# A decoder layer on one core: the q and k tables with the heads innermost, their low parts made later, and the routing spread out

## The reference

```python
# self attention: 16 heads of 8, relative logits from the unscaled queries
qkv = x @ qkv_w.T + qkv_b
logits = einsum('bhqd,bhkd->bhqk', q, k) * scale
pos = _rel_pos_logits(q_pos, rel_emb)            # [B*H, L, L], masked beyond +-99
out = einsum('bhqk,bhkd->bhqd', softmax(logits + pos), v) @ proj_w.T + proj_b
# cross attention: causal, k and v from ctx_1024, no biases
# experts: 64, top 8 of 4 kept groups of 8, relu(x @ up)^2 @ down, and a shared expert
x = layernorm(x + self_attention(x))
x = layernorm(x + cross_attention(x, ctx_1024))
x = layernorm(x + routed_experts(x) + shared_expert(x))
```

## Time and profile before

| What | Value |
|---|---|
| Median of 3 runs | 346.91 us |
| The profiled execution: time | 344.19 us |
| The profiled execution: span, first to last instruction | 342.4 us |
| Mean granted TensorE clock | 0.915 of 2.4 GHz |
| Busy: PE, DVE, ACT, POOL | 267.5, 228.3, 207.3, 141.0 us |
| Chain that ended last, by engine | PE 41%, DVE 18%, SP queue 12%, DMA 11%, issue 7%, POOL 5%, ACT 4% |
| Bytes moved | 41.09 MB in 55683 packets, of them 9.18 MB written to HBM |

### The profile page before, as it was taken

How to read it: one execution, slowest core, us unless ns; L and a number is a source line. 1 busy time by engine, 2 the same in 40 slices (tenths; PEclk the granted TensorE clock), 3 DMA queues, 4 the chain that set the end, 5 groups by cost and what they waited for, 6 DMA issues and landing times.

```text
span 342.4 us, 6024 instructions
## 1 busy us (share of the span) xinstructions
PE 267.5 (78%) x1904; PEld 210.6 (62%) x1904; DVE 228.3 (67%) x571; ACT 207.3 (61%) x573; POOL 141.0 (41%) x139
## 2 busy tenths in 40 slices
PE   2919999893069999998778775649969599999991
PEld 2608999572057887665555443538747488878870
DVE  2697854663038888986659989449999745674533
ACT  1502362774018888898767863346666578878861
POOL 7560000600000012244443500227569589879990
PEclk9976999998569999999989987688989899999997
DMA  6522225733432333465554100099547267658501
GB/s 113 144 97 104 102 103 180 172 83 130 154 105 64 94 94 92 93 158 149 149 167 136 50 0 3 15 225 253 138 124 171 73 163 179 174 160 215 142 0 31
DMA packets 55683, 41.09 MB, mean 120 GB/s; under 512 B 15394, under 2 KB 44772, under 8 KB 55652
## 3 DMA queue, kind: packets, MB, share of 16 engines
q1 hardware_dynamic: 55652, 40.71, 43.7%
HBM read 31.52 MB, written 9.18 MB: 119 GB/s over the span
## 4 chain that ended last, share of the span: by engine, by line
PE 41%; DVE 18%; SPq 12%; DMA 11%; issue 7%; POOL 5%; ACT 4%; POOLq 0%; DVEq 0%; ACTq 0%
PE bank L683 14%; PE bank L667 9%; SPq L417 6%; DMA qc_dram<-q_lo 5%; POOL unit_lo L594 5%; PE bank L718 4%; PE bank L700 4%; DVE spread L1086 3%; SPq L398 2%; DMA k_bd<-k_dram 2%; SPq L413 2%; PE bank L728 2%; DVE scaled L1262 2%; PE bank L706 2%; PE bank L739 1%
## 5 line engine op out<-in xcount | busy, mean ns | idle before, releaser
L594 POOL TENSOR_TENSOR unit_lo<-unit,unit_hi 128x512 fp32r<-128x512 f32 x68 | 87.3, 1303 | 48.7 <-ACT unit_hi L993 47.5
L916 ACT ACTIVATE probs<-bank,neg_max 128x128 f32<-128x128 f32 x256 | 72.3, 390 | 29.1 <-DVE neg_max L1123 28.1
L1262 DVE SCALAR_TENSOR_TENSOR scaled<-bank,roots 128x512 f32<-128x512 f32 x64 | 43.4, 686 | 30.2 <-PE bank L683 22.5
L1123 DVE TENSOR_REDUCE neg_max<-bank 128x4 f32<-128x512 f32 x64 | 42.9, 683 | 29.6 <-PE bank L706 29.0
L992 ACT ACTIVATE unit<-scaled 128x512 f32<-128x512 f32 x68 | 42.7, 628 | 32.8 <-DVE scaled L1262 30.5
L718 PE MATMUL bank<-ident,probs 128*128 128x128 f32 x256 | 39.9, 279 | 3.3 <-DVE probs_t L1130 2.4
L993 ACT ACTIVATE unit_hi<-scaled 128x512 fp32r<-128x512 f32 x68 | 41.9, 616 | 0.0
L718 PEld LDWEIGHTS bank<-ident,probs 128*128 128x128 f32 x256 | 30.5, 145 | 10.5 <-issue 5.2
L561 POOL CAST q_hi<-q_t 128x128 fp32r<-128x128 f32 x8 | 2.3, 293 | 83.6 <-ACT q_t L963 83.6
L706 PE MATMUL bank<-k_bd,q_stk 128*128 128x512 f32 x64 | 34.6, 540 | 0.0
L1130 DVE COPY probs_t<-bank 128x512 f32<-128x512 f32 x40 | 27.5, 687 | 10.4 <-PE bank L718 9.7
(11 more groups left out here) (176 smaller groups left out, 480.6 us busy)
## 6 DMA issues: line engine op xcount, KB each, us to landing
roots<-root_dram SPq DMA_DIRECT2D x64, 256.0 KB, 4.6
q_stk<-q_dram SPq DMA_DIRECT2D x8, 256.0 KB, 3.6
k_bd<-k_dram SPq DMA_DIRECT2D x32, 64.0 KB, 3.0
incoming<-in_L_ffn_up_w SPq DMA_DIRECT2D x4, 512.0 KB, 5.3
q_stk<-qc_dram SPq DMA_DIRECT2D x8, 256.0 KB, 3.0
k_bd<-kc_dram SPq DMA_DIRECT2D x32, 64.0 KB, 2.4
incoming<-in_L_ffn_down_w SPq DMA_DIRECT2D x4, 512.0 KB, 4.8
q_dram<-q_hi SPq DMA_DIRECT2D x4, 256.0 KB
```

Of the source, the lines that this page charges most:

```text
L594: nc.gpsimd.tensor_tensor(unit_lo[:, k % R], unit[:, k % 3], unit_hi[:, k % R], ALU.subtract).then_inc(lo_ready, 1)
L916: last = nc.scalar.activation(probs[:, U % 3, h4 * L:(h4 + 1) * L], ps[BS[U % 3]][:, h4 * L:(h4 + 1) * L], ACT.Exp, bias=neg_max[:, U % 4, ...
L1123: nc.vector.tensor_reduce(neg_max[:, U % 4, :], ps[BS[U % 3]][:, :].rearrange("p (h j) -> p h j", h=GH), AX.X, ALU.max, negate=True).then_ ...
L1262: ins = nc.vector.scalar_tensor_tensor(scaled[:, k % 3], h, 0.0, roots[:, n % ROOT_RING, c % ROOTS], ALU.max, ALU.mult)
```

## The change

**Order of the rows.** The 128 output features of q and k were ordered (head within group, feature, group). They are now ordered (feature, head within group, group), so that in the tables the 16 heads stand innermost. The reordering copies of weights, biases, masks and embeddings take the same elements in another order.

**Tables.** The tables of q are now (2, 128, tokens) and those of k (4, 128, tokens): q's parts are stored once each, not twice, and each store writes 128 plain rows. A gather reads q in two DMAs of 64 rows into the two halves of `q_stk`, and k in four DMAs, each into every fourth partition of `k_bd`.

**Who splits, and when.** ScalarE makes the high parts of the self stage for all columns after its last copy of the preparation (`q_high`, `k_high`). GpSimd makes the low parts, also for all columns at once, and first waits for `spread_ready` to reach 2, that is for the parts 0 and 1 of `q_spread`. The stores wait for these, one whole table after the other; the gather of sequence 0 waits for all.

**SyncE's list.** Gather 2 stands before the two loads of pieces. The stores of the context keys stand behind gather 3 (high parts) and gather 4 (low parts), no longer before gather 3.

**Routing.** Batch 2 gets 1.2 parts per step in place of 1.75, batch 3 starts four steps later, and the second turning of weights comes one step after the last part, not two: step 96 in place of 93.

```diff
-BATCHES = [(range(0, 2), 2), (range(2, 4), 3.5), (range(4, 6), 1.75), (range(6, 8), 1.2)]
+BATCHES = [(range(0, 2), 2), (range(2, 4), 3.5), (range(4, 6), 1.2), (range(6, 8), 1.2)]
+ROUTE0[3] += NG
-CT = [ROOTS_AT[1], ROOTS_AT[3] + 2]
+CT = [ROOTS_AT[1], ROOTS_AT[3] + 1]
...
-        q_dram, k_dram, qc_dram, kc_dram = (
-            nc.dram_tensor(f"{n}_dram", (GH, REPS, HD * NG, NB * L), F32, kind="Internal").ap()
-            for n in ("q", "k", "qc", "kc"))
+        q_dram, qc_dram = (nc.dram_tensor(f"{n}_dram", (2, D, NB * L), F32, kind="Internal").ap() for n in ("q", "qc"))
+        k_dram, kc_dram = (nc.dram_tensor(f"{n}_dram", (REPS, D, NB * L), F32, kind="Internal").ap() for n in ("k", "kc"))
...
-            def keep(store, parts, cols, kept):
-                for part, what in enumerate(parts):
-                    sp.dma_start(store[:, part, :, cols], what[:, cols]).then_inc(kept, 16)
-            def keep_queries(store, hi, lo, cols, kept):
-                keep(store, (hi, lo, hi, lo), cols, kept)
-            def keep_keys(store, hi, lo, cols, kept):
-                keep(store, (hi, hi, lo, lo), cols, kept)
+            def keep(store, parts, what, cols, kept):
+                for part in parts:
+                    sp.dma_start(store[part, :, cols], what[:, cols]).then_inc(kept, 16)
...
-                sp.dma_start(q_stk[r][:, :, :].bitcast(F32),
-                             queries[:, :, :, cols].rearrange("h s (d g) t -> (h s d) g t", g=NG))\
-                    .then_inc(stack_here[r], 16)
+                for rep in range(2):
+                    sp.dma_start(q_stk[r][rep * 64:(rep + 1) * 64, :, :].bitcast(F32),
+                                 queries[:, :, cols].rearrange("s (d h g) t -> (s d h) g t", h=GH, g=NG))\
+                        .then_inc(stack_here[r], 16)
                 for h4 in range(GH):
-                    sp.dma_start(k_bd[r][ROWS * h4:ROWS * (h4 + 1), :, h4, :].bitcast(F32),
-                                 keys[h4, :, :, cols].rearrange("s (d g) t -> (s d) g t", g=NG))\
+                    sp.dma_start(k_bd[r][h4::GH, :, h4, :].bitcast(F32),
+                                 keys[:, :, cols].rearrange("s (d h g) t -> h (s d) g t", h=GH, g=NG)[h4])\
                         .then_inc(stack_here[r], 16)
...
-            for f in range(2):
-                cols = slice(f * HT, (f + 1) * HT)
-                sp.wait_ge(q_split, 2 * (f + 1))
-                keep_queries(q_dram, q_hi, q_lo, cols, q_kept[f])
-                sp.wait_ge(k_split, 2 * (f + 1))
-                keep_keys(k_dram, k_hi, k_t, cols, k_kept[f])
-            sp.wait_ge(q_kept[0], 16 * REPS)
-            sp.wait_ge(k_kept[0], 16 * REPS)
+            every = slice(0, NB * L)
+            sp.wait_ge(q_high, 1)
+            keep(q_dram, (0,), q_hi, every, q_kept)
+            sp.wait_ge(k_high, 1)
+            keep(k_dram, (0, 1), k_hi, every, k_kept)
+            sp.wait_ge(q_split, 1)
+            keep(q_dram, (1,), q_lo, every, q_kept)
+            sp.wait_ge(k_split, 1)
+            keep(k_dram, (2, 3), k_t, every, k_kept)
+            sp.wait_ge(q_kept, 16 * 2)
+            sp.wait_ge(k_kept, 16 * REPS)
             sp.wait_ge(zeroed, 2)
             gather(0)
             gather(1)
             sp.wait_ge(zeroed, 3)
+            gather(2)
             load_piece(0)
             load_piece(1)
-            gather(2)
-            sp.wait_ge(q_kept[1], 16 * REPS)
-            sp.wait_ge(k_kept[1], 16 * REPS)
-            sp.wait_ge(k_split, 6)
-            keep_keys(kc_dram, k_hi, kc_t, slice(0, NB * L), kc_kept)
             for B in range(RING, 2 * NB):
...
-                    sp.wait_ge(qc_kept[B % 2], 16 * REPS * ((B - NB) // 2 + 1))
+                    sp.wait_ge(qc_kept[B % 2], 16 * 2 * ((B - NB) // 2 + 1))
                 gather(B)
+                if B == RING:
+                    sp.wait_ge(k_split, 3)
+                    keep(kc_dram, (0, 1), k_hi, every, kc_kept)
+                if B == RING + 1:
+                    keep(kc_dram, (2, 3), kc_t, every, kc_kept)
                 if 0 <= B - 7 < NB:
                     b = B - 7
+                    cols = slice(b * L, (b + 1) * L)
                     sp.wait_ge(qc_split, 2 * (b + 1))
-                    keep_queries(qc_dram, q_hi, q_lo, slice(b * L, (b + 1) * L), qc_kept[b % 2])
+                    keep(qc_dram, (0,), q_hi, cols, qc_kept[b % 2])
+                    keep(qc_dram, (1,), q_lo, cols, qc_kept[b % 2])
...
+            pool.wait_ge(spread_ready, 2)
+            pool.wait_ge(q_high, 1)
+            nc.gpsimd.tensor_tensor(q_lo[:, :].bitcast(F32R), q_t[:, :], q_hi[:, :], ALU.subtract).then_inc(q_split, 1)
+            pool.wait_ge(k_high, 1)
+            nc.gpsimd.tensor_tensor(k_t[:, :].bitcast(F32R), k_t[:, :], k_hi[:, :], ALU.subtract).then_inc(k_split, 1)
...
+            act.wait_ge(out_a, out_count("k1", False))
+            nc.scalar.copy(q_hi[:, :].bitcast(F32R), q_t[:, :]).then_inc(q_high, 1)
+            nc.scalar.copy(k_hi[:, :].bitcast(F32R), k_t[:, :]).then_inc(k_high, 1)
```

More of the change, by code:

```diff
@@ L296, in decoder_layer @@
         qc_split = sem("qc_split")
-        k_kept = [sem(f"k_kept{n}") for n in range(2)]
-        q_kept = [sem(f"q_kept{n}") for n in range(2)]
+        k_kept = sem("k_kept")
+        q_kept = sem("q_kept")
+        q_high = sem("q_high")
+        k_high = sem("k_high")
         qc_kept = [sem(f"qc_kept{n}") for n in range(2)]
@@ L523, in _ @@
             nc.gpsimd.memset(glist[:, :, TOPG:8], -3.0e38).then_inc(consts_made, 1)
-            for f in range(2):
-                cols = slice(f * HT, (f + 1) * HT)
-                pool.wait_ge(out_a, out_count(f"q{f}", False))
-                nc.gpsimd.tensor_copy(q_hi[:, cols].bitcast(F32R), q_t[:, cols]).then_inc(q_split, 1)
-                pool.wait_ge(q_split, 2 * f + 1)
-                nc.gpsimd.tensor_tensor(q_lo[:, cols].bitcast(F32R), q_t[:, cols], q_hi[:, cols], ALU.subtract)\
-                    .then_inc(q_split, 1)
-                pool.wait_ge(out_a, out_count(f"k{f}", False))
-                nc.gpsimd.tensor_copy(k_hi[:, cols].bitcast(F32R), k_t[:, cols]).then_inc(k_split, 1)
-                pool.wait_ge(k_split, 2 * f + 1)
-                nc.gpsimd.tensor_tensor(k_t[:, cols].bitcast(F32R), k_t[:, cols], k_hi[:, cols], ALU.subtract)\
-                    .then_inc(k_split, 1)
+            pool.wait_ge(spread_ready, 2)
[3 more added lines that the diff above has]
+            nc.gpsimd.tensor_tensor(k_t[:, :].bitcast(F32R), k_t[:, :], k_hi[:, :], ALU.subtract).then_inc(k_split, 1)
             pool.wait_ge(ld["x0"], 16)
@@ L546, in _ @@
             pool.wait_ge(out_a, sum(not by_vector(t) for t in TASKS))
-            for f in range(2):
-                pool.wait_ge(k_kept[f], 16 * REPS)
+            pool.wait_ge(k_kept, 16 * REPS)
             nc.gpsimd.tensor_copy(k_hi[:, :].bitcast(F32R), kc_t[:, :]).then_inc(k_split, 1)
-            pool.wait_ge(k_split, 5)
+            pool.wait_ge(k_split, 2)
             nc.gpsimd.tensor_tensor(kc_t[:, :].bitcast(F32R), kc_t[:, :], k_hi[:, :], ALU.subtract).then_inc(k_split, 1)
@@ L558, in _ @@
                     if b == 0:
-                        for f in range(2):
-                            pool.wait_ge(q_kept[f], 16 * REPS)
+                        pool.wait_ge(q_kept, 16 * 2)
                     nc.gpsimd.tensor_copy(q_hi[:, cols].bitcast(F32R), q_t[:, cols]).then_inc(qc_split, 1)
@@ L694, in scores @@
                 if g == 0:
-                    pe.wait_ge(stack_here[r], 16 * (1 + GH) * (B // RING + 1))
+                    pe.wait_ge(stack_here[r], 16 * (2 + GH) * (B // RING + 1))
                 if U < NU:
@@ L890, in _ @@
             for c in range(2):
-                nc.scalar.copy(wc_t[:, c, :].rearrange("p (h d g) -> p h d g", h=GH, g=NG),
-                               done("w_cross")[:, c * D:(c + 1) * D].rearrange("p (h g d) -> p h d g", h=GH, g=NG))
+                nc.scalar.copy(wc_t[:, c, :].rearrange("p (d h) -> p h d", h=H),
+                               done("w_cross")[:, c * D:(c + 1) * D].rearrange("p (h d) -> p h d", h=H))
             nc.scalar.copy(wc_t[:, 2:4, :].rearrange("p c d -> p (c d)"), done("w_cross")[:, 2 * D:4 * D])\
@@ L904, in _ @@
                                    done(f"bias{n}").rearrange("p (i r) -> p r i", i=4)).then_inc(out_a, 1)
-            for f in range(2):
-                act.wait_ge(k_kept[f], 16 * REPS)
+            act.wait_ge(k_kept, 16 * REPS)
             nc.scalar.mul(kc_t[:, 0:HT], done("kc0"), SCALE).then_inc(out_a, 1)
@@ L961, in queries_out @@
                     if b == 0:
-                        act.wait_ge(q_split, 4)
+                        act.wait_ge(q_split, 1)
                     nc.scalar.copy(q_t[:, b * L:(b + 1) * L], ps[BX][:, 0:L]).then_inc(qc_out, 1)
```

22 lines of the change are left out of this document (10 added, 12 removed).

## The result

The changed kernel takes 315.14 us (median of 4 runs, 313.45 to 316.58) against 346.72 (median of 4, 345.05 to 347.46) for the kernel before: a ratio of 0.9094, interval 0.9036 to 0.9151. The prediction was 312, with a range of 303 to 325. The profiled execution took 316.58 (span 314.8), so between the two profiled executions the difference is 27.6 us; in the medians it is 31.6. The medians given for a run are of all its executions; the ratios leave out an execution over 1.5% above its kernel's fastest, so a ratio need not be the quotient of two medians.

The account below looks back on a forecast made before the run. It took the kernel as bound by a slow start, a stop at 79 to 97 us, cross-stage rounds and VectorE's routing; 10.1 + 18.5 + 5.1 + 1.0 = 34.7 us off 346.9 gave 312 us, range 303 to 325.

Parts of the forecast that it names:

- Low parts later: Start: part 0 of `q_spread` falls to 4.28 us without GpSimd beside it, bias tasks begin at 20.3 to 20.4; gain 10.1 us.
- The added wait: Start: stores and gather 0 move later, stores at 250 GB/s, gather 0 lands at 43.4 us; nothing lost.
- My other end: Bound for the start's stores: at 104 GB/s they last 30 us, gather 0 lands near 60.4, taking back 9 us.
- Context keys: Stop from 79 to 97 us goes with the key stores behind gathers 3 and 4; gain 18.5 us.
- The cross stage: Units 40 to 56: rounds of 7.0 to 7.2 us, last store landing in 2.7 us; gain 5.1 us.
- Units 56 to 63: Stretch behind the cross stage's unit 56, without a term of its own in the prediction; change 0.
- Routing spread out: Experts: last root at least 2.8 us later, dense rest 4.3 us shorter; gain 1.0 us taken.
- Slow stores: Rival: stores stay at 104 GB/s, rows spread no wider; gain 18 in all, 329 us; chance 0.09.
- slow gather: Rival: gather of k into every fourth partition runs on one DMA engine, 26 GB/s; 362 us; chance 0.04.
- a part 0 that stays long: Rival at the start: part 0 of `q_spread` stays at 12 us for reasons other than GpSimd; 320 us; chance 0.03.
- The landing: Rival in the cross stage: last store's landing stays at 3.75 us, round 8.0, gain 1.5; 316 us; chance 0.11.
- Roots: Rival in the experts: second half's roots miss unit 36 by 3 us; 315 us; chance 0.05.

Follow-up runs that it names:

- the old plan: Changed kernel with the earlier kernel's routing (batch 2 at 1.75 parts per step, batch 3 not shifted, turn at step 93): 313.62 us, ratio 0.9076.
- the keys first: Changed kernel with both context-key stores put back ahead of gather 3: 315.93 us, ratio 0.9136.
- the best version: Changed kernel with the earlier routing of batches 2 and 3, turn at step 93, and batch 0 one step later: 310.97 us, repeated at 312.72 us.
- the later slot: Changed kernel with batch 0 of the routing one step later, all work kept: 313.28 us, ratio 0.9031.

## Why the prediction was right, point by point

*Low parts later: right (10.1 predicted, 9.65 measured).* The wait alone in the kernel before gives the same 4.30 us. The bias tasks began 1.0 us later than the 20.35 of my sum: the four early products took 3.65 us, not 2.74 (2.51 to 3.75 in the profiled runs made here), and TensorE waited 1.01 us for `ctx_t`, where I had counted 0.68. The bias tasks themselves then took 0.44 less, 28.85 for 29.29. Part 2 of `q_spread` was stretched by 0.97 us to 5.26, where I had 1.4, and hidden.

*The added wait: right in kind, the rate mis-sized.* I took 250 GB/s from loads and gathers; the stores ran at 386 to 445, four times the 104 of before. Gather 0 was issued at 32.5, not 37. It cost nothing either way. My other end, 9 us taken back at 104 GB/s, was for the 3.1 MB of the changed kernel. The experiment with the wait alone has 4.2 MB to store, and there the first scores came 11.1 us later although the bias tasks began 9.7 earlier: 20.8 taken back, of which the megabyte more is 10 by an estimate at 104 GB/s. No run had the narrow stores with 3.1 MB. The Trainium skill's rule of the largest divisor ("DMA: Bandwidth & Descriptors", "Why a DMA increments its semaphore by 16 and not by 1") gave 4 and 16 engines, and 2 and 9 tenths agree with it.

*Context keys: right (18.5 predicted, 18.9 measured).* But of the two edits that I put together here, the width is enough for most: 14.9 us in the kernel before, and only 1.5 us come back when the keys' place is undone. What the place would do without the width is open.

*The cross stage: right (5.1 predicted; 5.5 measured from unit 40 to 56, with 0.3 lost ahead of it), with the landing of the last store mis-sized.* I took 2.7 us between bounds of 2.2 and 3.75 and measured 1.71 to 1.77, below the lower one. It changed nothing, since the round was by then that of TensorE and ScalarE, busy 26.7 and 26.5 of the 28.96 us (VectorE 23.0): 6.76 and 7.03 us for the first two rounds, 7.97 for the last. The section "Anatomy of one DMA" of the Trainium skill ("DMA: Bandwidth & Descriptors"), with about 2 us of fixed time, was nearer than my row, though it too lies a little above. That section is written for DMAs that GpSimd issues; these are SyncE's.

*Units 56 to 63: missed (0 predicted, 3.0 lost).* The step that failed stands nowhere in the prediction as a term: I counted the cross stage to unit 56 and let the rest follow. I had asked of each faster piece what comes late next, but not what it now meets. SyncE loads a weight piece after most rounds, and with SyncE's rounds no longer the bound the loads come earlier against the units: that of piece 7 was issued 0.6 us behind unit 56 (182.95) and is now issued 2.9 us ahead of it (145.80). Its split then lay 6.8 us behind unit 56 and stretched `x_tok`'s affine step, with no TensorE wait on that step; now it lies 2.8 us behind and stretches the first routing step, in front of `o_norm`, which TensorE waits for. Taking the split away gives 2.6 us of the 3.0 back. Moving the routing by one slot gives 3.7, more than was lost, which fits a wait of TensorE for gather 15 in the kernel before (1.93 us) that is gone now. That is shown for the stretch. Of the 19.3 us about 2.3 go with the clock behind the hold, by the run with the old plan, which had the hold at a clock of 1.00.

*Routing spread out: wrong sign (gain 1.0 predicted, 2.8 lost).* The last root came 5.6 us later, the upper end of 2.8 + 4 x 0.7: 3.6 us more VectorE time, 2.8 of them the four units, and 2.2 more idle (in windows 0.2 longer). The tail was to be 4.3 shorter and was 2.8 shorter. Of the missing 1.5, TensorE's clock behind the longer wait for the last root makes 1.05: 2.1 us more at half speed. Of the 2.8, spreading itself costs 0.8 by the run with the old plan; the other 2 come with either plan, and their cause is open. The step that failed is the assumption that VectorE's own work and at most 0.7 us for each meeting with GpSimd set the time to the last root, with the tail shorter by all three steps.

Sum: 9.65 + 18.9 + 5.1 - 3.0 - 0.25 - 2.8 = 27.6. My profiled forecast was 309.5 and the profiled execution took 316.58; the median came to 315.14, 3.1 above the 312, because this time the profiled execution is the slowest of the runs, not the fastest.

*The rivals.* Slow stores, slow gather and a part 0 that stays long are excluded by the rows above. The gather of k into every fourth partition lands in 2.4 us (median of 32), not 3.0, and in the cross stage in 2.6, where it was 2.4. The landing did not stay at 3.75. Roots were not late.

## What to carry to other kernels

Look for stores at a flat rate with few DMA engines busy. Here stores with 4 rows outermost ran at 99 to 106 GB/s with 2 tenths busy, and those with 128 rows at 386 to 445 with 9 tenths; widen such stores first. Then work that had to be done early can be done late, and an edit that loses alone can win with others: the wait alone made the kernel 2.8% slower, the whole change 9% faster. When a stage gets faster, list what is issued from the same queue (here the loads of weight pieces, and so their splits on GpSimd), and see which instructions of the other engines each of those now meets.

## What the hardware showed that I had not expected

- Stores from SBUF to HBM on 16 engines run at 386 to 445 GB/s, against 225 to 292 for this kernel's gathers and loads.
- A `TENSOR_SCALAR` of VectorE that is issued during a GpSimd `TENSOR_TENSOR` or cast lasts until that one ends, in every instance looked at here: `r_one` ended at 153.90, the split of piece 7 at 153.82, 2.14 us for 0.22 of work. In the kernel before, the split of piece 6 (180.36, 2.36 us) held `x_tok`'s step (181.10, 1.71 us), ends at 182.72 and 182.81, and that of piece 7 the next one. `r_one` at 0.84 and 1.15 us in other runs is the same, only issued later: its ends follow those of the cast and the split by 0.08 us. So do the 16 steps of part 0 in the kernel before (the view of the tile `spread`, with shortest, median and longest in ns):

```profile
L1086 DVE TENSOR_SCALAR spread<-q_t,head_mask x16: 336/686/2426, 12.2 to 24.0; 128x256 f32<-128x256 f32 x16
```

  The 2426 ns are one step beside the last and longest GpSimd instruction, 2.39 us. Beside the four casts of 0.61 to 0.68 us the steps last about 0.69, beside the four subtractions of 1.27 about 1.43, and behind 22.36, with GpSimd idle, 0.34. So a string of short steps beside a string of long ones goes at one step for each GpSimd instruction. The Trainium skill ("SBUF — State Buffer", "Who interferes with whom") describes an exclusive lock on a port pair for a whole instruction, and these agree with it. The `RECIPROCAL` behind `r_one` took 0.95 us with and without GpSimd beside it.
- The granted clock behind the pause of TensorE near 154 us fell to 0.50 for 6 to 7 us in all three profiles of the changed kernel (waits of 2.44 to 2.88 and then 0.36 to 0.50 us), and for some 3 us without the split of piece 7 (1.53 and 0.50), with the keys first (2.86 and 0.50) and in the best version's second profile (2.41). It stayed at 1.00 in the old plan (2.34 and 0.50), the later slot (2.21) and the best version's first (1.46). So the length of the wait alone doesn't sort them. Behind the last root, 5.95 us of waiting were followed by 4.7 us at 0.50, 3.61 by 2.6 us, and 2.19 by none.
